# Rows of attention maxima: one transpose and a DMA, or four transposes a bank and a copy into row 96

## The reference

```python
Q, K, V = layernorm(x) @ Wq.T + bq, ctx @ Wk.T + bk, ctx @ Wv.T + bv   # split into 16 heads of 16
dot = einsum('bhsd,bhtd->bhst', Q, K) / sqrt(16)                        # 100 x 361 per head and batch
x = x + tanh(g_xattn) * (softmax(dot, -1) @ V joined) @ Wh.T + bh       # then the second layer
```

## Time and profile before

| what | us |
|---|---|
| median of 3 executions | 523.17 (521.51 to 524.47) |
| the profiled execution, its own time | 524.91 |
| its span, from first to last instruction | 523.1 |
| around the span | 1.8 |
| opening part, up to the first `pv_unit` of step 0 | 53.3 |
| steps 1 to 14, from there to the `pv_unit` of step 14 | 199.9 |
| last step and second layer | 269.9 |

### The profile page before, as it was taken

The page is one execution under the profiler, slowest core; times in us unless marked ns, Lnnn a source line. Parts: engine busy times, 40 slices in busy tenths (PEclk is TensorE's granted clock), DMA queues, the critical chain, the costliest instruction groups (busy, mean ns, idle before and its releaser), DMA issues.

```text
span 523.1 us, 11849 instructions
## 1 busy us (share of the span) xinstructions
PE 494.6 (95%) x4392; PEld 464.0 (89%) x4392; DVE 347.8 (66%) x761; ACT 271.0 (52%) x592; POOL 297.1 (57%) x350
## 2 busy tenths in 40 slices
PE   8879999999897999999998999999999999999995
PEld 7658999889897989898888999999999999999993
DVE  5857787778575877887557769665476456664443
ACT  4476766666465666667674532544335323433331
POOL 6564566665363666552769956644386434844441
PEclk9999999999898999999999999999999999999998
DMA  7685786887677587765111000010000100001001
GB/s 203 182 267 142 193 208 151 183 191 174 126 174 183 150 193 178 157 140 113 20 18 17 0 1 1 1 33 1 0 1 1 33 2 0 1 1 33 1 1 31
DMA packets 50729, 45.84 MB, mean 88 GB/s; under 512 B 33967, under 2 KB 40147, under 8 KB 50672
## 3 DMA queue, kind: packets, MB, share of 16 engines
q1 hardware_dynamic: 40270, 20.82, 17.6%
q0 software_dynamic: 8128, 21.05, 16.1%
q10 hardware_dynamic: 2274, 3.21, 1.9%
HBM read 20.59 MB, written 6.66 MB: 52 GB/s over the span
## 4 chain that ended last, share of the span: by engine, by line
PE 76%; DMA 10%; DVE 5%; ACT 3%; issue 2%; POOL 1%; SPq 1%; POOLq 0%; DVEq 0%; ACTq 0%
PE bank L1326 12%; PE bank L1188 7%; PE bank L1378 6%; DMA QS<-crow 6%; PE bank L1205 6%; PE bank L1343 6%; PE bank L1218 6%; PE bank L1330 6%; PE bank L1170 5%; PE bank L1358 4%; PE bank L1158 3%; PE bank L1251 2%; PE bank L1361 2%; DMA xs<-x 2%; PE bank L1292 2%
## 5 line engine op out<-in xcount | busy, mean ns | idle before, releaser
L943 DVE TENSOR_REDUCE nmax<-bank 100x1 f32<-100x361 f32 x256 | 130.5, 530 | 50.1 <-PE bank L1188 44.5
L409 POOL TENSOR_TENSOR awl<-hb,awh 128x400 fp32r<-128x400 f32 x64 | 70.5, 1103 | 101.9 <-ACT awh L622 101.9
L522 ACT ACTIVATE pt<-bank 120x400 f32<-120x400 f32 (+1 forms) x192 | 90.5, 502 | 33.2 <-PE bank L1205 19.2
L622 ACT ACTIVATE awh<-hb 128x400 fp32r<-128x400 f32 x64 | 34.5, 538 | 119.5 <-DVE hb L889 119.2
L1188 PE MATMUL bank<-KS,QS 96*100 96x362 f32 x256 | 87.2, 360 | 4.9 <-DVE nmax L943 4.4
L882 DVE TENSOR_TENSOR hb<-sil,bank 128x400 f32<-128x400 f32 x64 | 36.5, 570 | 82.8 <-PE bank L1343 38.8
L1205 PE MATMUL bank<-QS,KS 97*120 97x200 f32 (+1 forms) x384 | 68.0, 276 | 6.9 <-DMA QS<-crow 6.9
L318 POOL TENSOR_TENSOR cth<-craw,cth 128x724 fp32r<-128x724 f32 x16 | 27.7, 1730 | 71.6 <-ACT cth L468 65.7
L1205 PEld LDWEIGHTS bank<-QS,KS 97*120 97x120 f32 (+1 forms) x384 | 60.0, 187 | 9.3 <-DMA QS<-crow 8.3
L1188 PEld LDWEIGHTS bank<-KS,QS 96*100 96x100 f32 x256 | 42.1, 168 | 13.1 <-DVE nmax L943 6.2
L889 DVE TENSOR_TENSOR hb<-hb,wbT 128x400 f32<-128x400 f32 x64 | 47.7, 745 | 2.1
(11 more groups left out here) (197 smaller groups left out, 1120.9 us busy)
## 6 DMA issues: line engine op xcount, KB each, us to landing
KS<-kn SPq DMA_DIRECT2D x128, 90.5 KB, 2.8
KS<-kn POOLq DMA_DIRECT2D x64, 90.5 KB, 3.8
craw<-ctxT POOLq DMA_DIRECT2D x14, 361.0 KB, 5.9
QS<-q_dram POOLq DMA_DIRECT2D x92, 50.0 KB, 4.3
q_dram<-qn ACTq DMA_DIRECT2D x4, 400.0 KB, 4.2
o_dram<-on SPq DMA_DIRECT2D x16, 100.0 KB
xr<-o_dram SPq DMA_DIRECT2D x16, 100.0 KB
y<-xs SPq DMA_DIRECT2D x16, 100.0 KB
```

What stands on the lines that cost most here:

```text
L409: nc.gpsimd.tensor_tensor(awl[:, g % 2, slot], hb[:, slot], awh[:, g % 2, slot].bitcast(F32), ALU.subtract).then_inc(m["p_awl"], 1)
L522: nc.scalar.activation(pt[0:TW[t], u, :], pT[u % 3][0:TW[t], 0:CS], ACT.Exp, scale=float(DH) ** -0.5).then_inc(m["act_e"], 1)
L943: nc.vector.tensor_reduce(nmax[:, pos:pos + 1], pS[h % 2][0:S, 0:T], AX.X, ALU.max, negate=True).then_inc(m["dve_s"], 1)
```

## The change

The eight-column transpose, the tile `crow` and the DMA go. Each group of four heads now has four transposes of one column of `nmax` each, all into partition 0 of one bank, at columns 0, 100, 200 and 300, and ScalarE copies these 1 x 400 values straight into row 96 of `QS`. There are four such groups a batch. Their banks are `pO`, `pP[1]`, `pP[0]`, `pO` for groups 0 to 3. `st_unit` waits for ScalarE's copy of its own group instead of for a DMA. The orders of TensorE, ScalarE and VectorE around it are rewritten: in a step, `st_unit` 0 and 1 move behind the fourth `s_head`, unit 11 moves ahead of the last part of V, and that part moves between the last two `s_head`.

```diff
-        crow = sba("crow", [H // 2, 2, S], F32R)
-        row_bank = lambda b, half: ps[0] if (b, half) == (B - 1, 1) else pP[(1, 0)[half]]
+        row_bank = lambda b, g: ps[0] if (b, g) == (B - 1, 2) else (pP[1] if b == 0 else pO, pP[1], pP[0], pO)[g]
...
-            def row_out(b, half):
-                row_copy(b, half)
-                row_send(b, half)
...
-                act.dma_start(QS[b % 3][96:97, 2 * half:2 * half + 2, :, :, :].rearrange("o a b c d -> o (a b c d)").bitcast(F32),
-                              crow[:, half, :].bitcast(F32)).then_inc(m[("cr_a", "cr_b")[half]], 16)
+            def row_out(b, g):
+                act.wait_ge(m["pe_cT"], 4 * b + g + 1)
+                nc.scalar.activation(QS[b % 3][96:97, g, :, :, :].rearrange("o b c d -> o (b c d)"), row_bank(b, g)[0:1, 0:CS],
+                                     ACT.Copy).then_inc(m["act_c"], 1)
...
-                row_out(i, 1)
+                row_out(i, 2)
+                row_out(i, 3)
                 expo(i, 0)
...
                 expo(i, 6)
-                row_copy(i + 1, 0)
+                row_out(i + 1, 0)
                 expo(i, 7)
+                row_out(i + 1, 1)
...
                 expo(i, 9)
-                row_send(i + 1, 0)
...
+            def row_turn(b, g):
+                pe.wait_ge(m["dve_s"], H * B if (b, g) == (B - 1, 2) else H * b + 4 * g + 4)
+                if row_bank(b, g) is pO:
+                    wait(pe, "act_o", b if g == 3 else b - 1)
+                    if b and g == 0:
+                        pe.wait_ge(m["act_c"], 4 * b)
+                for k in range(4):
+                    last = nc.tensor.transpose(row_bank(b, g)[0:1, k * S:(k + 1) * S], nmax[:, 4 * g + k:4 * g + k + 1], ident[0:S, 0:S])
+                last.then_inc(m["pe_cT"], 1)
...
-                if u == 0:
-                    wait(pe, "cr_a", 16 * (b + 1))
-                if u == UN // 2:
-                    wait(pe, "cr_b", 16 * (b + 1))
+                if t == 0:
+                    pe.wait_ge(m["act_c"], 4 * b + q + 1)
```

More of the change, by code:

```diff
@@ L568, in _ @@
             q_high(2, 1)
+            row_out(0, 1)
             v_out(1, 0)
@@ L939, in head @@
                 dve.wait_ge(m["pe_s"], n + 1)
-                if h % 8 == 0:
-                    wait(dve, "pe_cT", 2 * b - 1 + h // 8)
+                if h % 4 == 0:
+                    wait(dve, "pe_cT", 4 * b - 3 + h // 4)
                 pos = h // 4 * 4 + h % 2 * 2 + h % 4 // 2
@@ L1002, in body @@
                 head(i + 1, 3)
+                head(i + 1, 4)
                 if has_k(i):
                     k_low(b, 0)
-                head(i + 1, 4)
                 head(i + 1, 5)
@@ L1008, in body @@
                     k_low(b, 1)
+                head(i + 1, 6)
                 if has_o(i):
                     shares(i)
-                head(i + 1, 6)
                 head(i + 1, 7)
@@ L1225, in o_turn @@
                 else:
-                    wait(pe, "act_c", min(2 * i + 1, 2 * B))
+                    wait(pe, "act_c", min(4 * i + 2, 4 * B))
                     wait(pe, "dve_x1", i - 2)
@@ L1234, in on_turn @@
                 if has_s(i):
-                    wait(pe, "act_c", 2 * i + 3)
+                    pe.wait_ge(m["act_c"], 4 * i + 6)
                 elif has_o(i):
@@ L1433, in _ @@
             s_head(0, 9)
+            pe.wait_ge(m["act_c"], 1)
+            row_turn(0, 1)
             pe.wait_ge(m["dve_kl"], 4)
@@ L1457, in body @@
                 wait(pe, "act_v", min(NT * (i + 2), NT * B))
-                wait(pe, "act_c", 2 * i)
-                row_turn(i, 1)
-                st_unit(i, 0)
+                wait(pe, "act_c", 4 * i)
+                row_turn(i, 2)
                 s_head(i + 1, 1)
@@ L1468, in body @@
                     k_part(b, 0, 0, 3)
+                row_turn(i, 3)
                 s_head(i + 1, 2)
@@ L1473, in body @@
                 s_head(i + 1, 3)
+                st_unit(i, 0)
+                st_unit(i, 1)
+                s_head(i + 1, 4)
                 if has_k(i):
-                    pe.wait_ge(m["act_c"], 2 * i + 2)
+                    pe.wait_ge(m["act_c"], 4 * i + 3)
                     k_part(b, 1, 0, 3)
-                s_head(i + 1, 4)
-                st_unit(i, 1)
                 if has_k(i):
@@ L1482, in body @@
                 st_unit(i, 2)
+                st_unit(i, 3)
+                s_head(i + 1, 6)
                 if has_o(i):
                     o_turn(i)
-                st_unit(i, 3)
                 st_unit(i, 4)
-                s_head(i + 1, 6)
+                s_head(i + 1, 7)
                 if i == B - 2:
                     token_turn(0, 0)
-                s_head(i + 1, 7)
                 st_unit(i, 5)
@@ L1494, in body @@
                     v_part(b, 0, 0, 3)
+                st_unit(i, 6)
+                if has_k(i):
                     v_part(b, 0, 3, 6)
-                st_unit(i, 6)
                 s_head(i + 1, 8)
                 st_unit(i, 7)
+                row_turn(i + 1, 0)
                 s_head(i + 1, 9)
@@ L1517, in body @@
                 st_unit(i, 9)
+                if has_y(i):
+                    on_turn(i)
                 st_unit(i, 10)
                 s_head(i + 1, 12)
+                st_unit(i, 11)
                 if has_k(i):
@@ L1528, in body @@
                 s_head(i + 1, 14)
+                if has_k(i):
+                    v_part(b, 2, 3, 6)
                 s_head(i + 1, 15)
@@ L1534, in last_step @@
                 pe.wait_ge(m["act_v"], NT * B)
-                pe.wait_ge(m["act_c"], 2 * i)
-                row_turn(i, 1)
+                pe.wait_ge(m["act_c"], 4 * i)
+                row_turn(i, 2)
                 st_unit(i, 0)
```

26 lines of the change are left out of this document (9 added, 17 removed).

## The result

The changed kernel takes 537.01 us as the median of 4 executions (536.70 to 538.64), the kernel before 523.62 beside it. The ratio is 1.0267, with a 95% interval from 1.0209 to 1.0324: slower by some 13 us. The forecast was slower, 531, with a range up to 537.0; the measured time lies just outside, and the loss is 13.4 us where the sum gave 7 to 8. In diffs and rows, `...` marks what is left out.

A forecast was written before the change was run, and what follows sets the result against it. TensorE, busy 95% of the span, was taken as the bound. Transposes 19.2, hidden 2.0, removed waits and half clock 11.8, new wait 1.4 gave +6.8 us on 524.91, 531.7; it said 531, range 524 to 537.

The forecast's parts named there:

- The transposes: On TensorE, four one-column transposes a group cost 0.35 us (0.20 to 0.35); 1.2 us more a batch, 19.2 in all.
- What goes: In the steps, 8.3 us of DMA waits with the weight-load bubble and 3.5 of half clock go, 11.8 together.
- The new wait at unit 11: Unit 11 waits for ScalarE's exponential 8: 0.1 us in each of 14 steps (0 to 0.3), 1.4 us.
- the last copy is queued ahead of nothing that an engine lacks at that time: In ScalarE's queue late in a step, the last copy of maxima was said to delay no engine.
- "No bound" for ScalarE: ScalarE's busy time rises from 9.2 to 10.7 us in a step of over 14, so it doesn't bound the step.
- What hides it: In step 14 and the opening, TensorE's waits for VectorE's maxima hide 2.0 us of the transposes, from 0 to 4.4.
- The sum: Over the whole kernel, 19.2 - 2.0 - 11.8 + 1.4 = +6.8 us.
- Cheap transposes: Rival: on TensorE one column turns in 0.05 us, 9.6 us in all, giving 521.7 to 523.1 us; chance 0.13.
- The new wait in each step: Rival: the chain to the first part of V slips, 14 steps lose about 0.4 each, +5.6, 537 us; chance 0.15.
- Waits that are worth more than counted: Rival: steps hold some 2 us more, and 4.4 us of VectorE waits may cover turns: 525 to 527; chance 0.12.
- The stretches that the prediction derived from it: In the steps, turns in place of waits would keep the half-clock stretches and their 3.5 us, 535; chance 0.03.
- The prediction's other ground: In the opening, the clock rose while only 34 transposes ran, so groups of four do not starve it.

The follow-up runs named there:

- e2: The kernel before with each eight-column transpose made eight times into the same place, 16 a batch, DMA and order kept: 539.85 us, ratio 1.0270.
- e3: The changed kernel with unit 11 moved behind the first three matmuls of the third part of V: 531.93 us, ratio 1.0123.
- e1: The changed kernel with one transpose a group in place of four, ScalarE still copying 400 values: 531.49 us, ratio 1.0122.
- e7: As e1, with ScalarE copying only 100 of the 400 values, three of four heads left unshifted: 522.61 us, ratio 0.9965.
- e10: As e3, with maxima and identity as fp32r and an ordinary matmul in place of each fp32 transpose: 530.66 us, ratio 1.0139.
- e4: The kernel before, still by DMA, second half of the maxima in two pieces, heads 8 to 11 sent a step earlier: 521.83 us, ratio 0.9883.
- e9: As e4, with the turn of xr behind units 9 and 10 and its load ahead of the last two K groups: 518.49 us, ratio 0.9878.

## Why the prediction was right and wrong

**The transposes: right.** Forecast 0.35 a group and 1.2 us a step; measured 0.35 and, in e2, 1.23. (The forecast's own rows give 0.29 + 0.05 = 0.34; its 0.06 was rounded up.)

**What goes: right, a little small.** The waits and the half-clock stretches were put at 11.8 us. Steps 1 to 11 took 159.0 us before (53.31 to 212.35), 12.5 above eleven times 13.32. After the change they take 163.2 (56.27 to 219.50), which is eleven times 14.84. All of the 12.5 came back.

**The new wait at unit 11: the step that failed.** The wait was foreseen, and its size was wrong. It was put at 0.1 us in each of 14 steps, from 0 to 0.3, and is 0.30 (e3), the end of the bound: 3.8 us in place of 1.4. The rows of the changed kernel above show where the working fell short. It counted from the last matmul of the second part of V, which starts near 126.79 (126.55 and two thirds of 0.36). TensorE's side, 1.06 us to the place of unit 11, came out: 127.68 + 0.17 = 127.85. ScalarE's side was put at 1.1 and is 1.18: `v_out` starts at 127.19, behind a copy that ends at 127.16, in place of 0.32 after its matmul, and exponential 8 ends at 127.97. The forecast had read the 0.32 where ScalarE had stood idle. So the sentence that "the last copy is queued ahead of nothing that an engine lacks at that time" is wrong, by 0.08 us. Two pieces were put at nothing: 0.05 from the exponential's end to the start of unit 11, and 0.10 for its weight load, which is no longer hidden. 0.04 + 0.08 + 0.05 + 0.10 is 0.27 of the 0.30.

**"No bound" for ScalarE: half right.** Its busy time of 10.4 us in 14.84 bounds nothing, but its order does. e1, e7 and e10 show a chain of exponential, copy, exponential, copy, `v_out` that sets the step as soon as TensorE's part is shorter by 0.5 us.

**What hides it: too large, and by another way.** 2.0 us were taken as covered by waits for VectorE. Against the kernel before, steps 12 and 13 grew by 1.73 each, more than an undisturbed step. Step 14 grew by 0.87, and the part after it by 0.3 where two groups cost 0.6. So no more than some 0.6 of the cost is missing from the time. Step 0 is a full step and paid as well. But e1 shows that it is not the transposes that set steps 12 to 14. With twelve fewer they take 15.74, 15.44 and 13.97 us, where the changed kernel has 15.73, 15.44 and 13.98. In step 12 TensorE waits for VectorE's maxima instead; the rows are of the kernel before, the changed kernel and e1:

```profile
216.34 0.41 PE L1188 MATMUL bank<-KS,QS 96*100 96x362 f32 x1 [0.42 <-DVE nmax L943]
```

```profile
224.10 0.41 PE L1181 MATMUL bank<-KS,QS 96*100 96x362 f32 x1 [0.64 <-DVE nmax L936]
```

```profile
217.57 0.41 PE L1182 MATMUL bank<-KS,QS 96*100 96x362 f32 x1 [1.17 <-DVE nmax L937]
```

There is cover in these steps, but what covers is itself later. One of VectorE's small instructions ahead of the maxima takes 1.35 us in steps 12 and 13 of the changed kernel (from 221.00 and 236.73), and 0.45 in those of the kernel before (from 214.13 and 228.13). And narrow copies on ScalarE take 0.5 us off each of the three steps (e7: 15.24, 14.95 and 13.47). Why the instruction takes longer is not shown.

**The sum.** For steps 1 to 14 the terms gave some +5.4 (16.8 + 1.4 - 11.8 and about 1 hidden); measured +8.5. The difference is the wait at unit 11, 2.4, and the cover that brought nothing, 1, less the 0.7 that the removed waits gave above the forecast; 0.4 is not located. The opening adds 3.0: 1.7 is its half-clock stretch, which is luck, the other 1.3 is step 0. The rest adds 0.3. So the pair of profiles shows 11.8 us, and about 10 of these are the change by named terms. The medians show 13.4, because the profiled execution of before lies 1.3 above its median and that of the changed kernel 0.3 below. The four executions of before may have been low ones, which is not shown: its later medians, over 11 to 23 executions, are 525.19 to 525.48, 11.5 to 11.8 below 537.01.

**The rivals.** Cheap transposes are excluded by e2. The new wait in each step was real, but at unit 11 and not at the first part of V, which showed no wait. Waits that are worth more than counted did not come either: the removed ones gave 12.5 in place of 11.8, and some 0.6 was covered, less than the forecast's own 2.0. The Trainium skill, "TensorE: Matmul & The Clock Gate", Part 4, says that transposes don't count as TensorE being busy. The stretches that the prediction derived from it did not come: the steps of the changed kernel run at 1.00 throughout, though 16 of the 193 matmuls of each are these transposes. The prediction's other ground, that the clock rose in the opening while only transposes ran, rests on their pitch alone, 0.21 us each and then, from 7.60 on, some 0.1. The column of the granted clock is 1.00 from 1.50 to 7.60 us too, so it doesn't show the rise.

**Where the forecast looked and did not see.** The kernel before had its waits for `crow`, and behind the two longest its half-clock stretches, because one transfer of 3 KB was issued at the start of a step, and TensorE came to unit 6 some 5.3 us after its issue (125.17 to 132.61 less the wait of 2.17). The chain of before has the transfer, from 125.17 on for 7.39 us, and for 6.0 to 7.9 us in three other steps:

```profile
125.17 7.39 DMA QS<-crow
```

e4 and e9 take that away by sending earlier the maxima that exist earlier, for 0.1 us of TensorE a step. The change takes it away for 1.5.

## What to carry to other kernels

Where one engine is busy in the whole of an undisturbed step, price a cure in that engine's time before anything else: here 1.2 us a step, 1.5 with the new wait, bought back 1.0. A late transfer is first a question of when its data exist and which consumer needs them; splitting it so that the ready part goes a step earlier was worth more than removing it. When a wait goes, look for the transfer that is late next: here it was `xr`, from another queue. And in an engine's queue each inserted instruction delays all behind it: follow the order, not the busy share.

## What was not expected of the hardware

A transpose of fp32 costs 0.085 to 0.09 us for 100 moving columns with weights of 1, 8 or 128 columns. Four of them as fp32r matmuls cost 0.22 us in place of 0.35 (e10). A ScalarE copy of 1 x 400 takes 0.49 us, nearly as long as 128 x 400 (0.50). A matmul whose weight load has to wait costs 0.1 us more (0.30 for unit 11 in place of 0.20). And TensorE's clock fell to 0.50 for 3.4 us in the opening in some executions of a program and not in others. More idle time before it doesn't explain that: from 26 to 30 us TensorE was busy for 2.20 us in the first profile of before, whose clock stayed at 1.00, and for 2.43 in that of the changed kernel, whose clock fell between 28 and 30.
